# Cross-attention with sixteen heads and a routed feed-forward on one core: exponentials of 24 of 400 four-head steps on VectorE, eight passes with a spare PSUM bank, V stored once, half of the epilogue in the loop

## The chip, the cores and the metric

One core of a Trainium2 chip runs the whole program. The time is device microseconds of one execution; three runs of the kernel before gave 854.18, 855.53 and 856.58 us. One more execution, of 855.05 us, was profiled.

## The reference, cut to what matters

```python
def attention(query, key_value):            # 1024 x 128 queries (layer-normed x), 6404 x 96 context
    q, k, v = ...                           # 16 heads of 8 channels each
    attn = softmax(clip(einsum('bhqd,bhkd->bhqk', q, k) * 8 ** -0.5, -1e4, 1e4))
    return einsum('bhqk,bhkd->bqhd', attn, v) @ Wo + bo
def ffn(x):                                 # 1024 x 128, hidden 512, 8 experts, 2 taken
    main = gelu(x @ W1m + b1m) @ W2m + b2m
    gate_w, top_idx = top2(softmax(mean(x, 1) @ w_gate + b_gate))
    expert = sum over both of gate_w * (gelu(x @ W1e[i] + b1e[i]) @ W2e[i] + b2e[i])
    return a * main + (1 - a) * expert
x = x + attention(layernorm(x), ctx);  x = x + ffn(layernorm(x))
```

## The kernel before

**Opening.** The context is loaded, transposed on TensorE and projected to K and V. DVE splits K into a rounded part and a rest (`split_k`, ten segments of 5 key tiles of 128 keys), SP's queue stores the parts of a segment to `k_dram` (`store_k`, 2 DMAs) and loads them back in the order in which row-tiled matmuls want them (`load_k`, 8 DMAs, semaphore `kst_in[s]`). The same is done with Q (`load_q`, 16 DMAs for a group of four heads). There are two `kparts` buffers, and each load waits for the landing of its store. Segment 0 is handled ahead of the loop, segments 1 to 9 while the loop runs, in that order on SP's one queue, and after them the 32 small DMAs of the key tail (`load_k_tail`). A flag computed on the chip picks the fast path that is described here.

**Loop.** The 16 heads are four groups. A *step* is one key tile of 128 keys, four heads and 512 queries: four score matmuls (K=32 rows, on four row groups of the array, fp32r) give four chunks of 128x512 scores; ScalarE takes the exponential; four value matmuls (32 output columns each, on four column groups, fp32) add 8 value sums and the denominator of each head to a PSUM bank. Chunks are packed by three into a *tile* of 128x1536, for which PSUM has two buffers `ps` of three banks. Each group does 50 key tiles for both halves of the queries and a tail, which makes 134 tiles a group and 536 in all. The two remaining banks `po` hold the sums of the two halves. TensorE's order is written out: at tile t it issues the scores of tile t+2 once the exponential of tile t is done, and then the values of each step whose last chunk lies in tile t. ScalarE runs one ACTIVATE Exp per tile, with the scale and the bias as numbers in the instruction, into one of four `probs` buffers.

V is copied by DVE group by group into `region_v` with blocks of 32 columns per head (`refill`). The K of the next group is loaded over the old one segment by segment, once its scores are done. At the end of a group DVE copies the sums to `oraw`, TensorE turns them to tokens in a `ps` buffer, and DVE normalises (`group_to_tokens`, `normalise`).

**Epilogue.** In the last group the first half of the queries is finished early, and its output projection runs in the loop. After the loop stand the second half's projection, both layer norms, the first layer of the main network, the gate (with a table load for Exp), the loads of the two experts that were picked, their first and second layers, and the output. b2 is added by a matmul with one row for each of eight output tiles (L1010).

## Time and profile before

| | |
|---|---|
| median of three runs (lowest, highest) | 855.53 us (854.18, 856.58) |
| the profiled execution, its own time | 855.05 us |
| its span, from the first to the last instruction | 853.3 us |
| around the span | 1.75 us |
| busy ACT, PE, DVE | 775.5 us (91%), 751.9 us (88%), 80.0 us (9%) |
| exponentials of the loop (L430) | 536, busy 723.0 us, first at 55.15 us, over at 786.77 us |
| score and value matmuls of the loop | busy 268.9 us and 427.0 us |
| from the last exponential to the end | 66.5 us |

The busy time of an engine is the union of its instructions. An ACTIVATE is shown longer than the time between two starts, since neighbours overlap, so the cost of one in a stream is that distance. "Idle before" tells how long an engine stood and what released it.

### The profile page before, as it was taken

What the parts mean: (1) busy time and instruction counts of PE and PEld (TensorE: products, weight loads), DVE (VectorE), ACT (ScalarE), POOL (GpSimd) and SP (SyncE); (2) the same over time, 40 slices, a digit from 0 to 9 for tenths busy, and PEclk for the clock granted to TensorE, in tenths of its full rate; (3) what the DMA queues carried; (4) which work ended last, traced back from release to release, by engine and by line L of the source; (5) the groups of instructions that cost most, each with busy time, mean ns of one, the idle gap of its engine ahead of it and who ended that gap; (6) DMA issues with size and microseconds to landing.
All of it is one profiled execution on the core that took longest, in us unless ns stands there. A gap on an engine that the chain in (4) does not pass through costs nothing.

```text
span 853.3 us, 12912 instructions
## 1 busy us (share of the span) xinstructions
PE 751.9 (88%) x5352; PEld 241.4 (28%) x5352; DVE 80.0 (9%) x231; ACT 775.5 (91%) x636; POOL 21.8 (3%) x35
## 2 busy tenths in 40 slices
PE   3989888888898888888988888888988899888798
PEld 2652222222222222222222222222222223222467
DVE  6631220000010000000100000000100001000300
ACT  2769999999999999999999999999999999999450
POOL 9000000000000000000000000000000000000000
PEclk9999999999999999999999999999999999999799
DMA  5234441300011000011100011000000000000010
GB/s 176 82 103 121 118 130 25 81 16 16 17 41 28 20 17 17 16 24 24 36 21 16 17 22 26 16 17 16 17 1 1 2 1 1 1 1 1 3 50 25
DMA packets 20713, 29.04 MB, mean 34 GB/s; under 512 B 7830, under 2 KB 11276, under 8 KB 20652
## 3 DMA queue, kind: packets, MB, share of 16 engines
q1 hardware_dynamic: 19628, 27.40, 12.7%
q8 instruction: 44, 0.72, 0.4%
q0 software_dynamic: 480, 0.66, 0.3%
q10 hardware_dynamic: 544, 0.12, 0.1%
q14 instruction: 17, 0.14, 0.1%
HBM read 20.02 MB, written 8.13 MB: 33 GB/s over the span
## 4 chain that ended last, share of the span: by engine, by line
PE 42%; ACT 33%; issue 22%; DVE 1%; DMA 1%; SPq 0%; ACTq 0%
ACT region_ctxT L430 33%; PE po L913 19%; PE ps L894 12%; PE ps L995 3%; PE po L1007 3%; PE po L795 1%; PE ps L784 1%; DVE xn L514 1%; PE po L916 1%; DMA region_ctx<-in_ctx 1%; PE ps L772 1%; PE po L1010 0%; PE ps L896 0%; PE po L814 0%; PE ps L856 0%
## 5 line engine op out<-in xcount | busy, mean ns | idle before, releaser
L430 ACT ACTIVATE region_ctxT<-ps 128x1536 f32<-128x1536 f32 x536 | 723.0, 1675 | 8.6 <-PE ps L894 8.1
L913 PE MATMUL po<-region_ctxT,region_v 128*32 128x512 f32 x3200 | 427.0, 606 | 0.2 <-ACT region_ctxT L430 0.2
L894 PE MATMUL ps<-qst,region_k 32*128 32x512 f32 x1600 | 268.9, 493 | 76.1 <-ACT region_ctxT L430 75.9
L894 PEld LDWEIGHTS ps<-qst,region_k 32*128 32x128 f32 x1600 | 104.3, 181 | 445.8 <-ACT region_ctxT L430 436.9
L913 PEld LDWEIGHTS po<-region_ctxT,region_v 128*32 128x32 f32 x3200 | 63.0, 108 | 100.2 <-issue 97.3
L623 DVE COPY region_v<-vall 128x160 f32<-128x160 f32 x40 | 12.6, 318 | 405.8 <-PE po L913 402.5
L285 ACT ACTIVATE region_ctxT<-ps 96x512 f32<-96x512 f32 (+1 forms) x13 | 7.6, 582 | 13.5 <-PE ps L772 13.5
L772 PE MATMUL ps<-ident,region_ctx 128*96 128x128 f32 x50 | 9.4, 324 | 6.7 <-DMA region_ctx<-in_ctx 6.7
L658 DVE COPY region_kT<-po 128x512 f32<-128x512 f32 x2 | 1.4, 692 | 145.3 <-PE po L916 82.5
L784 PE MATMUL ps<-region_ctxT,wk_sb 96*128 96x512 f32 (+1 forms) x26 | 14.4, 652 | 0.0
L298 ACT ACTIVATE vall<-po 128x512 f32<-128x512 f32 (+1 forms) x13 | 7.5, 585 | 7.1 <-PE po L795 7.1
L995 PE MATMUL ps<-xnT,region_ctx 128*128 128x512 f32 x32 | 13.9, 592 | 0.0
L795 PE MATMUL po<-wv_sb,region_ctxT 97*128 97x128 f32 x100 | 12.7, 282 | 0.8 <-issue 0.5
L795 PEld LDWEIGHTS po<-wv_sb,region_ctxT 97*128 97x128 f32 x100 | 11.7, 191 | 2.1 <-issue 1.5
L459 ACT ACTIVATE region_v<-ps,b1s 128x512 f32<-128x512 f32 x8 | 5.5, 687 | 7.3 <-PE ps L995 7.3
L514 DVE TENSOR_SCALAR xn<-xres,mv,rstd 128x128 f32<-128x128 f32 x16 | 11.6, 1269 | 0.1
L995 PE MATMUL ps<-xnT,w1m_sb 128*128 128x512 f32 x16 | 10.1, 794 | 0.8 <-ACT xnT L446 0.8
L772 PEld LDWEIGHTS ps<-ident,region_ctx 128*96 128x96 f32 x50 | 7.1, 152 | 12.7 <-issue 9.3
L651 DVE COPY region_kT<-po 128x512 f32<-128x512 f32 x6 | 4.2, 692 | 59.4 <-PE po L916 59.4
L290 ACT ACTIVATE region_kT<-ps 128x512 f32<-128x512 f32 (+1 forms) x13 | 7.6, 587 | 2.2 <-PE ps L784 2.0
L1007 PE MATMUL po<-region_ctx,region_ctxT 128*128 128x128 f32 x64 | 9.2, 286 | 0.0
L543 DVE CAST kparts<-region_kT 128x640 fp32r<-128x640 f32 (+1 forms) x10 | 4.9, 491 | 43.5 <-DMA k_dram<-kparts 43.4
(163 smaller groups left out, 204.6 us busy)
## 6 DMA issues: line engine op xcount, KB each, us to landing
region_k<-k_dram SPq DMA_DIRECT2D x320, 40.0 KB, 1.9
k_dram<-kparts SPq DMA_DIRECT2D x18, 320.0 KB, 3.4
qst<-q_dram SPq DMA_DIRECT2D x64, 32.0 KB
region_ctx<-in_ctx SPq DMA_DIRECT2D x2, 624.0 KB, 8.5
q_dram<-region_k SPq DMA_DIRECT2D x2, 512.0 KB, 4.1
k_dram<-kparts SPq DMA_DIRECT2D x2, 322.0 KB, 3.3
region_ctx<-in_ctx SPq DMA_DIRECT2D x1, 576.0 KB, 6.8
xres<-in_x SPq DMA_DIRECT2D x1, 512.0 KB, 4.3
```

Source lines behind the costliest of these rows:

```text
L285: act.activation(ctxT[0:CK, a:b], bank(c % 3, CK, b - a), ACT.Copy).then_inc(ctxT_ready, 1)
L430: act.activation(probs[:, t % NPR, :], ps[slot_of_tile(t) % NSB][:, :], ACT.Exp, scale=SCALE).then_inc(exp_ready, 1)
L514: v.tensor_scalar(xn[:, t, :], xres[:, t, :], mv[:, t, 0:1], rstd[:, 3, t:t + 1], ALU.subtract, ALU.mult).then_inc(xn_ready, 1)
L623: v.tensor_copy(vst[:, t0:t1, :].rearrange("p t (j m) -> p t j m", j=GH)[:, :, :, 0:D], vall[:, t0:t1, g * GH * D:(g + 1) * GH * D].rearra ...
L772: last = tr(dst[:, at:at + P], ctx_sb[:, t, :], ident[:, :])
L784: mm(bank(3 + c % 3, P, b - a), wk_sb[:, :], ctxT[0:CK, a:b], start=True, stop=True).then_inc(k_psum, 1)
L795: last = mm(po[nth % 2][:, (t % 4) * P:(t % 4 + 1) * P], lhsT, wv_sb[:, :], start=True, stop=True)
L894: last = mm(dst, kst[r, kt * P:(kt + 1) * P], qst[r, g % 2, queries], start=True, stop=True)
L913: last = mm(po[half][QUAD * j:QUAD * (j + 1), :], vst[:, kt, QUAD * j:QUAD * (j + 1)], src, start=first, stop=last_one, skip_group_check=True)
L916: last = mm(po[half][:, :], vtail[:, :], src, start=first, stop=last_one, skip_group_check=True)
L995: mm(bank(n % 6), w, xnT[:, half * BANK:(half + 1) * BANK], start=True, stop=True).then_inc(hid_psum, 1)
L1007: last = mm(dst, hid[e % 2][:, cb, t * P:(t + 1) * P], w2[:, cb, :], start=(e == 0 and cb == 0 and t % 4 == 0), stop=False, skip_group_che ...
```

## The change

- **24 of the 400 steps** (`D_PLAN`: pass, key tile, the tiles at which its four score chunks are issued, the tile of its values) leave ScalarE. Their score matmuls go, one at a time and mostly four tiles apart, into the `po` bank that the current pass doesn't use, and DVE computes the exponential: `u` and `f` per chunk, and six instructions on a pair of chunks. ScalarE's tiles fall from 536 to 504.
- **Eight passes.** A pass is one group and one half of the queries, first all four groups for the first half, then again for the second. Sums alternate between the two `po` banks, and the other one is the spare bank; turning sums to tokens uses it too. K is loaded from `k_dram` seven times over instead of three, and all four groups of Q are kept (`load_q` for groups 1, 2 and 3 after segments 2, 3 and 4).
- **The constant C5** that DVE's polynomial leaves out is divided out of ScalarE's results too, by a bias in a tile `ebias` of 128x1. The scale moves in part into Q.
- **V once.** `evac_v` writes `v9`, 8 columns and a one per head, and values matmuls read 9 columns of it. `refill` goes. TensorE waits for the last V copy ahead of the first score.
- **Epilogue.** Projection, layer norm and the main network's first layer of the first half run in the loop, at tiles 255 to 266. Square roots and the gate's Exp become `pow` on POOL. The b2 sum is broadcast by one matmul and added by DVE to `xres`. The output is stored in three pieces.

```diff
+PASSES = [(g, half) for half in range(NHALF) for g in range(NG)]
+NP = len(PASSES)
+LAST_OF_HALF = [max(p for p, (_, h) in enumerate(PASSES) if h == half) for half in range(NHALF)]
...
+D_PLAN = [
+    (0, 49, (22, 26, 30, 34), 47),
+    (1, 24, (38, 42, 46, 50), 67),
+    (1, 34, (54, 58, 62, 70), 83),
...
+    (2, 24, (106, 110, 114, 118), 129),
...
+    (3, 34, (176, 180, 184, 194), 207),
...
+    (4, 24, (230, 234, 238, 242), 254),
+    (4, 39, (246, 272, 276, 280), 293),
...
+    (7, 49, (448, 452, 456, 460), 466),
+]
...
+STEPS = [(p, kt) for p in range(NP) for kt in range(FULL + 1) if kt not in DKT[p]]
+CHUNKS = [(n, j) for n, (_, kt) in enumerate(STEPS) for j in (range(GH) if kt < FULL else [None])]
+NT = len(CHUNKS) // CPT
...
+SPARE = sorted([(t, "score", GH * d + j) for d, (_, _, at, _) in enumerate(D_PLAN) for j, t in enumerate(at)]
+               + [(PASS_END[p] + NORM_GAP, "tokens", p) for p in range(NP - 1)])
...
+def pv_bank(p):
+    return p % 2
...
-                    if s == 2:
-                        load_q(sp, 1)
+                    if 2 <= s < 1 + NG:
+                        load_q(sp, s - 1)
...
-                for g in range(1, NG):
+                for p in range(1, NP):
                     for s in range(NSEG):
-                        chunks = (s + 1) * SEG_T * NHALF * GH if s < NSEG - 1 else CH_G
-                        sp.wait_ge(scores_ready, (g - 1) * TL_G + (chunks - 1) // CPT + 1)
-                        load_k(sp, g, s)
-                    if g + 1 < NG:
-                        load_q(sp, g + 1)
+                        sp.wait_ge(scores_ready, tile_of_segment(p - 1, s) + 1)
+                        if spare_of_segment(p - 1, s):
...
+                pool.memset(vtail[QUAD * j:QUAD * j + TAIL, :, QUAD * j + D:QUAD * j + V9], 1.0).then_inc(vones_ready, 1)
+            pool.wait_ge(vones_ready, 2 + GH)
+            pool.memset(powers[:, :], -0.5).then_inc(powers_ready, 1)
...
+            for n in range(NHALF):
+                pool.wait_ge(var_ready, 2 + n)
+                r = slice(n * QT // 2, (n + 1) * QT // 2)
+                pool.tensor_tensor(rstd[:, 3, r], rstd[:, 0, r], powers[:, 0:QT // 2], ALU.pow).then_inc(std_ready, 1)
+            pool.wait_ge(msum_ready, 2)
+            pool.tensor_tensor(gate[0:1, 2, :], euler[:, :], gate[0:1, 1, :], ALU.pow).then_inc(exp_gate, 1)
...
-                for t in range(NG * TL_G):
+                act.wait_ge(powers_ready, 3)
+                for t in range(NT):
                     act.wait_ge(scores_ready, t + 1)
                     if t >= NPR:
-                        g, i = divmod(t - NPR, TL_G)
-                        act.wait_ge(pv_done, g * QD_G + CHUNKS[g][CPT * i + CPT - 1][3] + 1)
-                    act.activation(probs[:, t % NPR, :], ps[slot_of_tile(t) % NSB][:, :], ACT.Exp, scale=SCALE).then_inc(exp_ready, 1)
+                        act.wait_ge(pv_done, values_through(t - NPR))
+                    act.activation(probs[:, t % NPR, :], ps[t % NSB][:, :], ACT.Exp, bias=ebias[:, 0:1],
+                                   scale=ESCALE).then_inc(exp_ready, 1)
+                if D_PLAN:
+                    act.wait_ge(d_ready, len(D_PLAN) * GH // 2)
...
+            act.wait_ge(pre_taken, CB)
+            act.activation(hid[0][:, :, 0:BANK], pre[:, :, :], ACT.Gelu_apprx_tanh).then_inc(main0_ready, 1)
...
+            def first_half_main(link):
+
+                take_first_attT()
+                residual(0, po[EPI_BANK][:, :], link)
+                dve.wait_ge(std_ready, 2)
+                scale_rows(halves[0])
+                dve.wait_ge(xnT_psum, NHALF + 1)
+                v.tensor_copy(xnT[:, 0:BANK], po[EPI_BANK][:, :]).then_inc(xnT_ready, 1)
+                dve.wait_ge(xnT_ready, NHALF + 1)
+                link(v.tensor_reduce(msum[:, 0:1], xnT[:, 0:BANK], AX.X, ALU.add))
+                for cb in range(CB):
+                    dve.wait_ge(pre_psum, cb + 1)
+                    v.tensor_scalar(pre[:, cb, :], po[EPI_BANK][:, :], b1T[:, E * CB + cb:E * CB + cb + 1], None,
+                                    ALU.add).then_inc(pre_taken, 1)
...
+                def take_sums(p):
+
+                    dve.wait_ge(pv_done, VALUES_OF_PASS[p][-1] + 1)
+                    v.tensor_copy(oraw[:, p % 2, :], po[pv_bank(p)][:, :]).then_inc(o_taken, 1)
...
+                    dve.wait_ge(spare_psum, n + 1)
+                    d_count(("u", c), v.tensor_scalar(du[:, i % 2, part], src, MAGIC, None, ALU.add))
+                    pair_until(i - 1, 1 + 3 * m)
+                    dve.wait_ge(d_step, d_mark["u", c])
+                    v.scalar_tensor_tensor(df[:, i % 2, part], du[:, i % 2, part], MAGIC, src,
+                                           ALU.subtract, ALU.subtract).then_inc(spare_taken, 1)
+                    pair_until(i - 1, 3 + 3 * m)
...
+                        if d_stage[i] == 1:
+                            dve.wait_ge(d_step, d_mark["u", 2 * i + 1])
+                            dve.wait_ge(spare_taken, SPARE_OF["score", 2 * i + 1] + 1)
+                            d_count(("e", i), v.tensor_scalar(u.bitcast(U32), u.bitcast(U32), 23, None, ALU.logical_shift_left))
...
+                            d_count(("q1", i), v.scalar_tensor_tensor(res, f, A1, f, ALU.add, ALU.mult))
+                        elif d_stage[i] == 3:
+                            d_count(("q2", i), v.scalar_tensor_tensor(q, f, A2, f, ALU.add, ALU.mult))
+                        elif d_stage[i] == 4:
+                            dve.wait_ge(d_step, max(d_mark["q1", i], d_mark["e", i]))
+                            d_count(("p1", i), v.scalar_tensor_tensor(res, res, B1, u, ALU.add, ALU.mult))
+                        elif d_stage[i] == 5:
+                            dve.wait_ge(d_step, max(d_mark["p1", i], d_mark["q2", i]))
+                            d_count(("p2", i), v.scalar_tensor_tensor(res, q, B2, res, ALU.add, ALU.mult))
+                        else:
+                            dve.wait_ge(d_step, d_mark["p2", i])
+                            v.scalar_tensor_tensor(res, f, R0, res, ALU.subtract, ALU.mult).then_inc(d_ready, 1)
...
+            dve.wait_ge(bsumb_psum, 1)
             for n in range(NHALF):
+                r = slice(halves[n].start, halves[n].stop)
+                v.tensor_tensor(xres[:, r, :], xres[:, r, :], bank(MIX_BANK)[:, P:2 * P].unsqueeze(1).broadcast_to([P, QT // 2, C]),
+                                ALU.add).then_inc(bsumb_taken, 1)
+            dve.wait_ge(bsumb_taken, NHALF)
+            for n, (t0, t1) in enumerate(OUT_TILES):
                 dve.wait_ge(ffn_psum, n + 1)
-                v.tensor_tensor(xn[:, n * QT // 2:(n + 1) * QT // 2, :],
-                                po[n][:, :].rearrange("p (t c) -> p t c", c=C),
-                                xres[:, n * QT // 2:(n + 1) * QT // 2, :], ALU.add).then_inc(res_ready, 1)
+                v.tensor_tensor(xn[:, t0:t1, :], [po[0], po[1], bank(4)][n][:, 0:(t1 - t0) * P].rearrange("p (t c) -> p t c", c=C),
+                                xres[:, t0:t1, :], ALU.add).then_inc(res_ready, 1)
...
+            def first_main(cb):
+
+                if cb == 0:
+                    pe.wait_ge(xnT_ready, NHALF + 1)
+                else:
+                    pe.wait_ge(pre_taken, cb)
+                mm(po[EPI_BANK][:, :], w1m_sb[:, cb * P:(cb + 1) * P], xnT[:, 0:BANK], start=True, stop=True).then_inc(pre_psum, 1)
...
+                    if (p, kt // SEG_T) not in seen:
+                        seen.add((p, kt // SEG_T))
+                        pe.wait_ge(kst_in[kt // SEG_T], 16 * GH * PARTS * (p + 1))
+                    r = slice(QUAD * j, QUAD * (j + 1))
+                    return mm(dst, kst[r, kt * P:(kt + 1) * P], qst[r, g, queries], start=True, stop=True)
...
+                def spare_job(n):
+
+                    t, kind, i = SPARE[n]
+                    if n:
+                        pe.wait_ge(spare_taken, n)
+                        if SPARE[n - 1][1:] == ("tokens", LAST_OF_HALF[0]):
+                            pe.wait_ge(pre_taken, CB)
+                    if kind == "tokens":
+                        pe.wait_ge(o_taken, i + 1)
+                        dst = po[1 - pv_bank(i + 1)]
+                        for a in range(QT // 2):
+                            last = tr(dst[:, a * P:(a + 1) * P], oraw[:, i % 2, a * P:(a + 1) * P], ident[:, :])
...
+                        d, j = divmod(i, GH)
+                        p, kt, _, _ = D_PLAN[d]
+                        last = scores(po[1 - pv_bank(pass_at(t))][:, :], p, kt, j)
+                    last.then_inc(spare_psum, 1)
...
+                    if first and p >= 1:
+                        used = sum(at <= t for at, _, _ in SPARE)
+                        if used:
+                            pe.wait_ge(spare_taken, used)
+                        if p >= 2:
+                            pe.wait_ge(o_taken, p - 1)
...
+                        if kind == 1:
+                            pe.wait_ge(d_ready, 2 * (i + 1))
+                        for j in range(GH):
+                            if kind == 0:
+                                tile, m = divmod(CHUNKS.index((i, j)), CPT)
+                                src = probs[:, tile % NPR, m * BANK:(m + 1) * BANK]
+                            else:
+                                src = dres[:, i % 2, j * BANK:(j + 1) * BANK]
+                            last = mm(dst[QUAD * j:QUAD * j + V9, :], v9[:, kt, GH * PASSES[p][0] + j, :], src,
...
+                pe.wait_ge(v_done, VCH)
+                pe.wait_ge(vones_ready, 1)
...
+                epilogue = PASS_END[LAST_OF_HALF[0]] + NORM_GAP
+                for t in range(NT):
+                    if t + NSB < NT:
                         score_tile(t + NSB)
+                    for n, (at, _, _) in enumerate(SPARE):
+                        if at == t:
+                            spare_job(n)
+                    if t == epilogue + EPI_AT[0]:
+                        pe.wait_ge(spare_taken, SPARE_OF["tokens", LAST_OF_HALF[0]] + 1)
+                        att_transpose(0, po[EPI_BANK])
+                    if t == epilogue + EPI_AT[1]:
+                        project_out(0, po[EPI_BANK])
+                    if t == epilogue + EPI_AT[2]:
+                        xn_transpose(0, po[EPI_BANK])
+                    if t - epilogue in EPI_AT[3:]:
+                        first_main(EPI_AT.index(t - epilogue) - 3)
```

Three places in the order of instructions, before and after. First **SP's queue** from the load of segment 2 (the second `region_k` group here) to the store of segment 5, before:

```order
L259 DMA region_k<-k_dram 16x640 x7
L280 DMA qst<-q_dram 8x1024 x16
L246 DMA k_dram<-kparts 16x8x640 [waits kparts_ready]
L246 DMA k_dram<-kparts 16x8x640
L259 DMA region_k<-k_dram 16x640 [waits kparts_stored1]
L259 DMA region_k<-k_dram 16x640 x7
L246 DMA k_dram<-kparts 16x8x640 [waits kparts_ready]
L246 DMA k_dram<-kparts 16x8x640
L259 DMA region_k<-k_dram 16x640 [waits kparts_stored0]
```

and now:

```order
L324 DMA region_k<-k_dram 16x640 x7
L343 DMA qst<-q_dram 8x1024 x16
L311 DMA k_dram<-kparts 16x8x640 [waits kparts_ready]
L311 DMA k_dram<-kparts 16x8x640
L324 DMA region_k<-k_dram 16x640 [waits kparts_stored1]
L324 DMA region_k<-k_dram 16x640 x7
L343 DMA qst<-q_dram 8x1024 x16
L311 DMA k_dram<-kparts 16x8x640 [waits kparts_ready]
L311 DMA k_dram<-kparts 16x8x640
L324 DMA region_k<-k_dram 16x640 [waits kparts_stored0]
L324 DMA region_k<-k_dram 16x640 x7
```

Behind the loads of segments 3 and 4 there now stand 16 more loads of Q each, ahead of the next store of K.

Second, **TensorE's queue** at the tiles 22 to 24 of the loop; `ps0` and `ps1` are the two score tiles, `po0` and `po1` the banks of sums. Before:

```order
L894 MATMUL ps0<-qst,region_k 128x512 x2
L894 MATMUL ps1<-qst,region_k 128x512 [waits exp_ready]
L894 MATMUL ps1<-qst,region_k 128x512 x2
L913 MATMUL po1<-region_ctxT,region_v 32x512 [waits exp_ready]
L913 MATMUL po1<-region_ctxT,region_v 32x512 x3
L894 MATMUL ps0<-qst,region_k 128x512 [waits exp_ready]
L894 MATMUL ps0<-qst,region_k 128x512 x2
L913 MATMUL po0<-region_ctxT,region_v 32x512 [waits exp_ready]
L913 MATMUL po0<-region_ctxT,region_v 32x512 x3
```

and now:

```order
L1022 MATMUL ps0<-qst,region_k 128x512 [waits exp_ready]
L1022 MATMUL ps0<-qst,region_k 128x512 x2
L1022 MATMUL po1<-qst,region_k 128x512 [waits kst_in9]
L1082 MATMUL po0<-region_ctxT,v9 9x512 [waits exp_ready]
L1082 MATMUL po0<-region_ctxT,v9 9x512 x3
L1022 MATMUL ps1<-qst,region_k 128x512 [waits exp_ready]
L1022 MATMUL ps1<-qst,region_k 128x512 x2
L1082 MATMUL po0<-region_ctxT,v9 9x512 [waits exp_ready]
L1082 MATMUL po0<-region_ctxT,v9 9x512 x3
L1022 MATMUL ps0<-qst,region_k 128x512 [waits exp_ready]
```

The score into `po1` is the first chunk of the first step of `D_PLAN`, key tile 49. It waits for `kst_in9`, and the values of tile 22 and all later scores of the loop stand behind it; the wait for `kst_in4` comes later in the queue.

Third, **TensorE's queue** at tile 38, now:

```order
L1022 MATMUL ps0<-qst,region_k 128x512 [waits kst_in6,exp_ready]
L1022 MATMUL ps0<-qst,region_k 128x512 x2
L1022 MATMUL po1<-qst,region_k 128x512 [waits kst_in4,qst_in1,spare_taken]
L1082 MATMUL po0<-region_ctxT,v9 9x512 [waits exp_ready]
L1082 MATMUL po0<-region_ctxT,v9 9x512 x3
L1022 MATMUL ps1<-qst,region_k 128x512 [waits exp_ready]
```

This chunk is the first of pass 1's key tile 24: it waits for the second load of segment 4, again ahead of the values and scores that follow. Before, no wait on that segment's second load stands ahead of the second group's own step.

**ScalarE's** exponential reads one more operand; before:

```order
L430 ACTIVATE region_ctxT<-ps0 128x1536 [waits pv_done,scores_ready]
```

and now:

```order
L501 ACTIVATE region_ctxT<-ps0,ebias 128x1536 [waits pv_done,scores_ready]
```

The operand `ebias` is the pointer to the 128x1 bias.

## Rows read from the trace of the kernel before

**Rows 1.** The page's costliest groups: busy us, mean ns of one, idle us before and its releaser.

```profile
L430 ACT ACTIVATE region_ctxT<-ps 128x1536 f32<-128x1536 f32 x536 | 723.0, 1675 | 8.6 <-PE ps L894 8.1
...
L894 PE MATMUL ps<-qst,region_k 32*128 32x512 f32 x1600 | 268.9, 493 | 76.1 <-ACT region_ctxT L430 75.9
```

**Rows 2.** Timeline of a steady stretch of the loop: start us, us, engine, line, count, idle before.

```profile
299.12 13.86 ACT L430 ACTIVATE region_ctxT<-ps 128x1536 f32<-128x1536 f32 x10
...
302.46 0.50 PE L894 MATMUL ps<-qst,region_k 32*128 32x512 f32 x3
...
302.90 1.07 PE L913 MATMUL po<-region_ctxT,region_v 128*32 128x512 f32 x8
```

**Rows 3.** Timeline of ScalarE in the opening, with pointer bias (L409, L411) and without.

```profile
26.53 0.68 ACT L411 ACTIVATE xn<-po,bqc 128x512 f32<-128x512 f32 x1
27.10 0.69 ACT L409 ACTIVATE qT<-po,bqc 128x512 f32<-128x512 f32 x1
...
28.33 0.59 ACT L285 ACTIVATE region_ctxT<-ps 96x512 f32<-96x512 f32 x1
28.81 0.60 ACT L290 ACTIVATE region_kT<-ps 128x512 f32<-128x512 f32 x1
```

**Rows 4.** Timeline of ScalarE in the epilogue, four Gelus with a pointer bias in a row.

```profile
809.50 2.42 ACT L459 ACTIVATE region_ctxT<-ps,b1T 128x512 f32<-128x512 f32 x4
```

**Rows 5.** Timeline of SP's queue: loads of K (L259), Q (L280), tail (L270), stores (L246).

```profile
65.46 3.55 SPq L259 DMA_DIRECT2D region_k<-k_dram  x8
69.06 5.40 SPq L280 DMA_DIRECT2D qst<-q_dram  x16
74.90 1.18 SPq L246 DMA_DIRECT2D k_dram<-kparts  x2
...
126.01 3.56 SPq L259 DMA_DIRECT2D region_k<-k_dram  x8
129.68 15.47 SPq L270 DMA_DIRECT2D ktail<-k_dram  x32
```

**Rows 6.** The page's DMA issues: KB each, us from issue to landing.

```profile
region_k<-k_dram SPq DMA_DIRECT2D x320, 40.0 KB, 1.9
```

**Rows 7.** Timeline where the loop begins.

```profile
54.70 0.49 ACT L298 ACTIVATE vall<-po 128x384 f32<-128x384 f32 x1 [0.55 <-PE po L795]
55.15 6.85 ACT L430 ACTIVATE region_ctxT<-ps 128x1536 f32<-128x1536 f32 x5
...
59.70 0.80 PE L894 MATMUL ps<-qst,region_k 32*128 32x512 f32 x3
...
60.43 1.94 PE L913 MATMUL po<-region_ctxT,region_v 128*32 128x512 f32 x8
...
63.01 4.22 ACT L430 ACTIVATE region_ctxT<-ps 128x1536 f32<-128x1536 f32 x3 [1.02 <-PE ps L894]
```

**Rows 8.** Windows: us, busy of PE, PEld, DVE, ACT, POOL, granted clock, DMA share, GB/s.

```profile
55.00:64.00 9.00, 6.75 (x45) 1.62 (x39) 3.33 (x7) 7.98 (x7) 0.00 (x0) 0.81 0.50 138
...
235.00:255.00 20.00, 18.41 (x133) 5.55 (x131) 3.04 (x9) 17.96 (x14) 0.00 (x0) 1.00 0.17 43
```

**Rows 9.** Groups by line and form, for the prices of DVE's work.

```profile
L535 DVE TENSOR_TENSOR region_k<-qT,region_k 128x1024 fp32r<-128x1024 f32 x1 | 1.2, 1226 | 0.0
...
L594 DVE TENSOR_TENSOR xres<-ps,xres 128x512 f32<-128x512 f32 x1 | 0.7, 692 | 4.0 <-PE ps L856 4.0
```

**Rows 10.** Timelines of the epilogue.

```profile
786.77 1.28 ACT L439 ACT_TABLE_LOAD   x1
...
806.60 1.28 ACT L471 ACT_TABLE_LOAD   x1
...
816.98 13.90 PE L995 MATMUL ps<-xnT,region_ctx 128*128 128x512 f32 x32
...
840.35 0.48 PE L1010 MATMUL po<-bsum,ones 1*128 1x128 f32 x2
...
840.76 1.16 PE L1007 MATMUL po<-region_ctx,region_ctxT 128*128 128x128 f32 x8
```

482 lines of the change are left out of this document (253 added, 229 removed).

## The prediction

> **What bounds the kernel now.** I read the page's costliest groups first. The loop's 536 exponentials are busy for 723.0 us, 1.349 us each, and ScalarE stood only 8.6 us before them; TensorE stood 76.1 us before its scores, nearly all of it for ScalarE [rows 1]. The loop is ScalarE's, by a small margin. The timeline of a steady stretch shows the margin: ten exponentials span 13.86 us. Taking off the last one's own length (the mean of 1.675 us in [rows 1], a little more here) leaves 1.34 to 1.35 us from start to start [rows 2], and I use 1.343. TensorE takes 0.44 us from its scores to its values, and the values of a step last 1.07 us, of which some 0.07 overlap with what follows [rows 2]. Four tiles carry three steps: 4 x 0.44 + 3 x 1.00 = 4.8 us against ScalarE's 5.37. So whoever takes work from ScalarE must leave its other tiles as fast as they are, and must not stop TensorE, whose queue is in order. Both are to be tested.
>
> **1. Fewer exponentials.** 32 tiles of 1.343 us go: 43.0 us less. This is the intended gain.
>
> **2. Each exponential gets dearer.** The instruction now reads its bias through a pointer. The trace has ScalarE with and without one, at 512 elements and in a stream: from L411 to the next L409, both with a pointer, 0.57 us from start to start; from L285 to L290, without, 0.48 [rows 3]. Four Gelus with a pointer take 2.42 us, (2.42 - 0.69) / 3 = 0.577 from start to start [rows 3, 4]. 512 elements are the same in all, so 0.09 us is per instruction, and nothing hides it, since ScalarE is the bound. Bounds: 0 (if the long instruction hides the read, as it already starts before its neighbour ends) and 0.097. I take 0.09, because the rows are of streams as well. 504 x 1.433 = 722.2 us, against 536 x 1.343 = 719.8: the gain of part 1 is used up.
> The Trainium skill's page "ScalarE: Activation LUTs", section "What ACT_TABLE_LOAD costs", gives an ACTIVATE without pointers 186 ns + 0.833 ns per element, about 93 ns more per pointer operand, and an overlap of about 93 ns between neighbours. By it one would cost an estimated 1.466 us and the loop some 17 us more than I sum; the trace has less distance than that today, so the measured one decides.
>
> **3. TensorE waits for a K segment that isn't there yet.** The spare score at tile 22 is key tile 49, in segment 9, and needs its first load. In the trace the loads of segment 9 are issued from 126.01 us on for 3.56 us, and a load lands 1.9 us after issue: there at about 131 us [rows 5, 6]. SP's queue sets this, with one segment after another through store, landing and load. It now has two more Q loads ahead: from the Q load at 69.06 to the next store at 74.90 are 5.84 us [rows 5], so 11.7 us twice over, less 0.2 us for the `refill` that DVE no longer has in front. Segment 9 is there at 142.6 us. When is tile 22? The first score waits for the last V copy, which ends at 54.70 + 0.49 = 55.2 us; with scores behind it the first exponential starts at 55.9 instead of 55.15 [rows 7]. The exponential of tile 22, after which the spare score stands, is over at 55.9 + 23 x 1.433 = 88.9 us, and with the scores that are already there ScalarE runs through tile 24 until 91.7. Then the values and scores behind the spare score have to come: at the low clock 0.5 + 1.94 + 0.8 us, as at the loop's start [rows 7], where the granted clock was 0.81 in the mean of a window [rows 8], thus partly at 1.2 GHz. Tile 25 starts at 145.5: **53.8 us** of idle ScalarE. Segments 4 to 8 arrive meanwhile, so nothing more waits in pass 0.
>
> **4. A second such wait.** At tile 38 the score of pass 1's key tile 24 wants the second load of segment 4. Behind segment 9, SP has the key tail, 129.68 + 15.47 us in the trace [rows 5], shifted by 11.5: until 156.7. Five segments of 3.55 us follow, until 174.4, landed at 175.9. TensorE has the scores through tile 40 issued, and ScalarE ends tile 40 at 145.5 + 1.0 (TensorE still cold, 1.02 us were lost so before [rows 7]) + 16 x 1.433 = 169.4; tile 41 starts at 178, and 1 us is lost again. Together **10.5 us** with the 1.0 of the first restart. The later spare scores come 6 to 36 tiles (8.6 us and more) after the scores that release their segment, and a load takes 3.55 + 1.9 us: no wait.
>
> **5. TensorE's margin.** Four tiles are now 5.73 us long, and hold 4.8 us as before, one spare score (0.2 to 0.43 us, from a third of [rows 2]'s 0.50 to all of it) and a quarter of a step's values (0.25): 5.2 to 5.5 us. It fits, but not evenly: 19 of the 24 steps put their values in a tile that has values already, 2.4 us of work in one tile. I take 0.2 us each, **5** (0 to 12). Each pass ends with a tail chunk and transposes. Three group ends cost 20.00 - 17.96 = 2.0 us each [rows 8]; seven ends with half the work, four of them with first values that wait for DVE's normalise in the same tile, I take at **8** (3 to 14) in all. Half an epilogue in the loop: transposes, projection and four 512-column matmuls of 0.86 us (13.90 us for 16 pairs [rows 10]) are some 6.4 us in 14 tiles that have 3.3 to spare: **3** (1 to 6).
>
> **6. DVE.** Per chunk it does two instructions from PSUM of 512 elements (0.69 us each) and three of 1024 (1.23 us each [rows 9]): at most 5.1 us in 5.73. ScalarE's loop hides it. If this cover goes, each 0.1 us over costs 9 us. Nine instead of 32 weight columns change nothing, since 512 columns are streamed as before and a step's four matmuls keep their four column groups; seven K loads instead of three lie beside the loop. Both cost nothing.
>
> **7. The end.** From the last exponential to the end are 66.5 us (853.3 - 786.8 [rows 10]). Up to the second half's layer norm all stays. Then TensorE is no longer in the first half's first layer, and the gate loses a table load of 1.28 us at 806.60 [rows 10] and gets POOL's `pow` instead, of which there is no row; I take it at half the table load, with 0 and 2 us as bounds. The experts' first layer, at 816.98, can start 2.7 us (1 to 4) sooner, when its weights have landed. Eight b2 matmuls go, 840.35 to 840.76 each [rows 10]: 3.3 us, and up to 4.7 without the breaks in the stream, I take 4.0. A smaller last output gives 0.3. End: **59.5 us** (57 to 63).
>
> **Sum.** 55.9 + 722.2 + 53.8 + 10.5 + 5 + 8 + 3 = 858.4 us for the loop's end; + 59.5 = 917.9 us of span; + 1.75 us around the span, as in the profiled execution of 855.05 us, gives **919.7 us**. That execution is 0.5 us under the median of 855.53, so I leave it at that.
>
> **Rivals.**
> A. The pointer's read is hidden in long instructions. For it: exponentials last 1.675 us and follow each other at 1.343, so 0.3 us overlap. Against it: [rows 3, 4]. Then 45.3 us less, the two waits begin sooner and last 3.6 us longer, and TensorE at 5.2 to 5.5 us of 5.37 becomes the bound, some 10 us: **888 us**.
> B. K arrives in time; the place is `kst_in9` at tile 22. For it: today TensorE waits for ScalarE alone ahead of its scores [rows 1]. Against it: the queue's dates, which no term of the change brings forward. It decides from the point at which segment 9 is there by 91.7 us; each us sooner gives one back, 64.3 in all: **855 us**, and with part 5's terms at their low ends 843, faster than before.
> C. DVE's chain of waits on its own results makes a chunk 6.2 us instead of at most 5.1: ScalarE waits by way of the spare bank in some 90 intervals, + 0.47 x 90: **962 us**. Against it: DVE's start gaps are small, and independent instructions lie between.
> D. The change does what it says, A and B at once: 919.7 - 64.3 - 45.3 + 10 = **820 us**.
>
> **How the numbers follow.** Forecast 0.74, A 0.10, B 0.04, C 0.08, D 0.02, and 0.02 for something else that is slower. The forecast's own range is 905 to 934, from the bounds in parts 2 to 7. To hold 8 in 10 the range must take in the better part of A: 884 to 934. About 0.3% is what this kernel's measurement can tell from no change: 853 to 858 us. Faster: D and half of B, 0.04; same: 0.02; slower: the rest, 0.94.
>
> **What the profile of the changed kernel would show.** Part 2: the exponential's busy time over its 504 instructions, 1.43 us against 1.349. Parts 3 and 4: two idle stretches of ScalarE, of some 54 and 9 us, released by a spare score that was released by a load of K; segment 9's loads issued until 141 us. Part 5: ScalarE's other idle time before L501 around 16 us. Part 6: DVE at 80 to 90% in the loop, with TensorE's waits on it short. Part 7: 59 to 60 us behind the last exponential. It would be wrong if SP's queue ran ahead of its dates, or if the pointer were free.

## The result, and the profile after

The changed kernel takes **923.53 us** (median of 4 runs, 923.22 to 925.35) against 855.31 us for the kernel before (4 runs): the ratio is 1.080, with a 95% interval of 1.078 to 1.082. The forecast was 919.7 us, the range 884 to 934. The profiled execution took 925.35 us, 1.8 us over the median, with a span of 923.6 us; the steps below are measured against the forecast span of 917.9 us.

The page's costliest groups of the kernel after (line, engine, operation, count, busy us, mean ns of one, idle us before and its releaser) answer to [rows 1]:

```profile
L501 ACT ACTIVATE region_ctxT<-ps,ebias 128x1536 f32<-128x1536 f32 x504 | 726.4, 1615 | 84.7 <-PE ps L1022 83.5
...
L1022 PE MATMUL po<-qst,region_k 32*128 32x512 f32 x96 | 40.4, 421 | 59.1 <-DMA region_k<-k_dram 59.1
```

Busy time over count is 726.4 / 504 = 1.441 us for an exponential, against 1.349 in [rows 1], and ScalarE's idle time before them has gone from 8.6 to 84.7 us. The second row is the spare scores: 59.1 us of TensorE's idle time before them, all for a load of K. The timeline of ScalarE (start us, length us, count, idle before and its releaser) shows where the idle time lies:

```profile
51.82 5.83 ACT L501 ACTIVATE region_ctxT<-ps,ebias 128x1536 f32<-128x1536 f32 x4 [0.66 <-PE ps L1022]
...
140.89 1.54 ACT L501 ACTIVATE region_ctxT<-ps,ebias 128x1536 f32<-128x1536 f32 x1 [50.96 <-PE ps L1022]
143.44 21.58 ACT L501 ACTIVATE region_ctxT<-ps,ebias 128x1536 f32<-128x1536 f32 x15 [1.01 <-PE ps L1022]
175.43 1.54 ACT L501 ACTIVATE region_ctxT<-ps,ebias 128x1536 f32<-128x1536 f32 x1 [10.41 <-PE ps L1022]
177.87 11.56 ACT L501 ACTIVATE region_ctxT<-ps,ebias 128x1536 f32<-128x1536 f32 x8 [0.90 <-PE ps L1022]
...
344.50 23.01 ACT L501 ACTIVATE region_ctxT<-ps,ebias 128x1536 f32<-128x1536 f32 x16 [0.28 <-PE ps L1022]
...
811.63 1.54 ACT L501 ACTIVATE region_ctxT<-ps,ebias 128x1536 f32<-128x1536 f32 x1 [3.44 <-PE ps L1022]
```

Two stretches, 50.96 us until 140.89 and 10.41 us until 175.43, are the forecast's waits for K. Each has a restart behind it (1.01 and 0.90 us). Sixteen exponentials in a row take 23.01 us and a lone one 1.54, so from start to start it is (23.01 - 1.54) / 15 = 1.431 us. In TensorE's timeline, the instruction that ends each wait is a spare score, and the matmuls behind it are slow:

```profile
137.50 0.79 PE L1022 MATMUL po<-qst,region_k 32*128 32x512 f32 x1 [49.81 <-DMA region_k<-k_dram]
138.22 1.90 PE L1082 MATMUL po<-region_ctxT,v 128*9 128x512 f32 x8
...
143.63 1.05 PE L1082 MATMUL po<-region_ctxT,v 128*9 128x512 f32 x8
...
172.07 0.76 PE L1022 MATMUL po<-qst,region_k 32*128 32x512 f32 x1 [9.29 <-DMA region_k<-k_dram]
```

The values of a step take 1.90 us there, as at the loop's start in [rows 7], against 1.05 a few microseconds later. Between 90 and 137 us TensorE did nothing and its granted clock was 0.50, that is 1.2 GHz. It was still 0.50 from 138 to 143 us, where the slow matmuls are, and from 185 us on it is 1.00 (windows: us, busy of PE, PEld, DVE, ACT, POOL, granted clock, DMA share, GB/s):

```profile
90.00:137.00 47.00, 0.00 (x0) 0.00 (x0) 6.96 (x20) 0.00 (x0) 0.00 (x0) 0.50 0.48 122
138.00:143.00 5.00, 5.00 (x24) 0.95 (x25) 1.38 (x2) 1.54 (x1) 0.00 (x0) 0.50 0.03 1
...
185.00:860.00 675.00, 597.73 (x4440) 151.54 (x4436) 426.55 (x499) 656.15 (x457) 1.04 (x1) 1.00 0.15 32
```

SP's queue (L311 stores of K, L324 loads of K, L343 of Q, L335 of the key tail) answers to [rows 5]. Three groups of Q loads of 5.4 us stand between K's segments (at 64.42, 79.46 and 92.51 us), where one stood before, and the loads of segment 9 begin at 132.40 instead of 126.01. The second loads of K follow from 152.01 us on:

```profile
79.46 5.38 SPq L343 DMA_DIRECT2D qst<-q_dram  x16
...
92.51 5.38 SPq L343 DMA_DIRECT2D qst<-q_dram  x16
...
132.40 3.55 SPq L324 DMA_DIRECT2D region_k<-k_dram  x8
...
152.01 44.82 SPq L324 DMA_DIRECT2D region_k<-k_dram  x64
```

### The profile page after: what moved, and what is told of

It is laid out like the page before. It is cut to its first block, busy times and chain, and to the rows that moved or that the text cites. A ratio compares the mean times of both kernels' runs of the same rounds, so it can differ in the third digit from the quotient of the medians.

```text
span 923.6 us, 13620 instructions
## 1 busy us (share of the span) xinstructions
PE 752.6 (81%) x5338; PEld 228.6 (25%) x5338; DVE 498.4 (54%) x669; ACT 772.9 (84%) x591; POOL 20.7 (2%) x37
## 4 chain that ended last, share of the span: by engine, by line
ACT 33%; PE 27%; issue 25%; SPq 7%; DMA 5%; DVE 3%; POOLq 0%; ACTq 0%; POOL 0%; DVEq 0%
ACT region_ctxT L501 33%; PE po L1082 12%; PE ps L1022 6%; SPq L324 5%; DMA k_dram<-kparts 3%; PE ps L1157 2%; SPq L343 2%; PE po L1176 1%; PE ps L914 1%; PE po L925 1%; PE po L1071 1%; DMA region_ctx<-in_ctx 1%; PE po L1022 1%; PE ps L902 1%; SPq L311 1%
## 5 line engine op out<-in xcount | busy, mean ns | idle before, releaser
L501 ACT ACTIVATE region_ctxT<-ps,ebias 128x1536 f32<-128x1536 f32 x504 | 726.4, 1615 | 84.7 <-PE ps L1022 83.5
L1082 PE MATMUL po<-region_ctxT,v 128*9 128x512 f32 x3008 | 399.1, 603 | 3.8 <-ACT region_ctxT L501 3.8
L736 DVE TENSOR_SCALAR region_kT<-po 128x512 f32<-128x512 f32 x96 | 66.4, 692 | 196.3 <-PE po L1022 196.3
L1022 PE MATMUL po<-qst,region_k 32*128 32x512 f32 x96 | 40.4, 421 | 59.1 <-DMA region_k<-k_dram 59.1
L1082 PEld LDWEIGHTS po<-region_ctxT,v 128*9 128x9 f32 x3008 | 44.8, 88 | 107.1 <-issue 96.3
L739 DVE SCALAR_TENSOR_TENSOR region_kT<-region_kT,po 128x512 f32<-128x512 f32 x96 | 65.3, 681 | 0.2
L770 DVE SCALAR_TENSOR_TENSOR dres<-region_kT,dres 128x1024 f32<-128x1024 f32 x48 | 58.8, 1225 | 1.6
L767 DVE SCALAR_TENSOR_TENSOR dres<-region_kT,dres 128x1024 f32<-128x1024 f32 x48 | 58.5, 1220 | 0.2
L759 DVE SCALAR_TENSOR_TENSOR dres<-region_kT 128x1024 f32<-128x1024 f32 x48 | 58.5, 1219 | 0.0
L761 DVE SCALAR_TENSOR_TENSOR region_kT<-region_kT 128x1024 f32<-128x1024 f32 x48 | 58.5, 1218 | 0.0
L764 DVE SCALAR_TENSOR_TENSOR dres<-dres,region_kT 128x1024 f32<-128x1024 f32 x48 | 58.4, 1216 | 0.0
L608 DVE CAST kparts<-region_kT 128x640 fp32r<-128x640 f32 (+1 forms) x10 | 4.9, 492 | 60.1 <-DMA k_dram<-kparts 59.1
L457 POOL TENSOR_TENSOR rstd<-rstd,powers 128x4 f32<-128x4 f32 x2 | 2.1, 1026 | 855.7 <-DVE rstd L562 855.7
```

What stands on the lines that cost most here:

```text
L501: act.activation(probs[:, t % NPR, :], ps[t % NSB][:, :], ACT.Exp, bias=ebias[:, 0:1], scale=ESCALE).then_inc(exp_ready, 1)
L736: d_count(("u", c), v.tensor_scalar(du[:, i % 2, part], src, MAGIC, None, ALU.add))
L739: v.scalar_tensor_tensor(df[:, i % 2, part], du[:, i % 2, part], MAGIC, src, ALU.subtract, ALU.subtract).then_inc(spare_taken, 1)
L759: d_count(("q1", i), v.scalar_tensor_tensor(res, f, A1, f, ALU.add, ALU.mult))
L761: d_count(("q2", i), v.scalar_tensor_tensor(q, f, A2, f, ALU.add, ALU.mult))
L764: d_count(("p1", i), v.scalar_tensor_tensor(res, res, B1, u, ALU.add, ALU.mult))
```

## The experiments

The theory was that of the prediction: the pointer eats the 32 exponentials that were saved, and SP's queue of loads makes TensorE, and with it ScalarE, wait twice. In the figures below, "the changed kernel" takes 923.5 us and the kernel before between 854.5 and 855.7 us, measured anew beside each set of runs.

### The pointer alone, in the kernel before

```diff
+            pool.memset(zbias[:, :], 0.0).then_inc(zbias_ready, 1)
...
-                    act.activation(probs[:, t % NPR, :], ps[slot_of_tile(t) % NSB][:, :], ACT.Exp, scale=SCALE).then_inc(exp_ready, 1)
+                    act.activation(probs[:, t % NPR, :], ps[slot_of_tile(t) % NSB][:, :], ACT.Exp, bias=zbias[:, 0:1], scale=SCALE).then_inc(exp_ready, 1)
```

> The kernel before, with one edit: its 536 exponentials read their bias (zero) through a pointer to a column of 128 values, as in the changed kernel. Theory (part 2: the read costs 0.09 us for each instruction, nothing hides it): stream spacing 1.343 -> 1.433 us, 536 x 0.09 = 48 us, 903 us in all (855 to 907 by the bounds). Rival A (the read is hidden in the long instruction): 855 us, within 0.3%.

Measured: **898.54 us** (896.03 to 899.07), ratio 1.052 (1.050 to 1.055). The page's row for the exponentials:

```profile
L434 ACT ACTIVATE region_ctxT<-ps,zbias 128x1536 f32<-128x1536 f32 x536 | 768.8, 1878 | 7.1 <-PE ps L898 7.1
```

768.8 / 536 = 1.434 us against 1.349. The 43.9 us between the medians are 0.082 us for each exponential, 0.080 to 0.087 by the interval. The timelines have 128 exponentials in one piece, first with the pointer, then in the kernel before:

```profile
261.42 183.41 ACT L434 ACTIVATE region_ctxT<-ps,zbias 128x1536 f32<-128x1536 f32 x128 [0.60 <-PE ps L898]
```

```profile
63.01 172.13 ACT L430 ACTIVATE region_ctxT<-ps 128x1536 f32<-128x1536 f32 x128 [1.02 <-PE ps L894]
```

Taking off a lone one's length (1.54 and 1.45 us), these are 1.432 and 1.344 us from start to start, 0.088 apart. So the price taken from instructions a third as long, 0.09 us, was right to 0.002 us for the distance in a stream, and 10% too high for the time. Part of the difference is idle time of ScalarE, which falls from 8.6 to 7.1 us; the rest wasn't taken apart. The pointer's read is not hidden in a long instruction, and rival A's condition is false. By the Trainium skill, page "ScalarE: Activation LUTs", section "What ACT_TABLE_LOAD costs", a pointer operand adds about 93 ns: the 0.088 us agree to within 0.01 us. Its level of 1.466 us does not: this run shows 1.432.

### The pointer taken out of the changed kernel

The added lines are POOL's; TensorE takes `v9d` instead of `v9` for the values of VectorE's steps.

```diff
-                    act.activation(probs[:, t % NPR, :], ps[t % NSB][:, :], ACT.Exp, bias=ebias[:, 0:1],
-                                   scale=ESCALE).then_inc(exp_ready, 1)
+                    act.activation(probs[:, t % NPR, :], ps[t % NSB][:, :], ACT.Exp, scale=ESCALE).then_inc(exp_ready, 1)
...
+            for i, kt in enumerate(DK):
+                pool.tensor_scalar(v9d[:, i, :, :], v9[:, kt, :, :], C5, None, ALU.mult).then_inc(v9d_ready, 1)
```

> The changed kernel without the pointer: the exponentials have no bias again, and the factor that the bias stood for is put on copies of V's columns for the six key tiles that VectorE's steps use. Theory (the pointer costs 0.082 us, as in the kernel before with a pointer, and the K waits' dates don't move, so that the 41 exponentials ahead of tile 41 gain nothing): 463 x 0.082 = 38 us less, 886 us, and up to 10 us more if TensorE becomes the bound at 5.2 to 5.5 us for four tiles of 5.37 (range 885 to 896). Rival (in the changed kernel ScalarE's spacing is set by something else, such as TensorE or DVE, and the pointer is hidden): 915 us or more.

Measured: **896.59 us** (895.62 to 897.16), 26.9 us less and just above the range. The rows of ScalarE, first the page's, then two of the timeline:

```profile
L504 ACT ACTIVATE region_ctxT<-ps 128x1536 f32<-128x1536 f32 x504 | 684.9, 1523 | 96.1 <-PE ps L1024 94.4
...
140.06 1.45 ACT L504 ACTIVATE region_ctxT<-ps 128x1536 f32<-128x1536 f32 x1 [52.45 <-PE ps L1024]
...
357.90 21.60 ACT L504 ACTIVATE region_ctxT<-ps 128x1536 f32<-128x1536 f32 x16 [0.63 <-PE ps L1024]
```

The exponentials' busy time falls by 726.4 - 684.9 = 41.5 us, 0.082 each (0.085 in the first experiment, and 0.088 here too from start to start: (21.60 - 1.45) / 15 = 1.343). Their idle time rises from 84.7 to 96.1 us. The two K waits (now 52.45 and 11.81 us) take 2.5 us of it with their restarts, since they end only 0.8 and 1.1 us sooner. The wait for the last step's values and its restart take 1.9 us (4.49 + 1.10 against 3.44 + 0.29). The other 7 us are TensorE's margin: behind most of VectorE's steps ScalarE stands about 0.6 us, where it stood 0.28 with the pointer (the 0.28 at 344.50 above). Rival A's 10 us for this were about right, and that the price comes in the tiles of a step's values too.

### Only the first step's key tile changed

```diff
-    (0, 49, (22, 26, 30, 34), 47),
+    (0, 4, (22, 26, 30, 34), 47),
```

> The changed kernel, with the key tile of the first VectorE step changed from 49 (segment 9) to 4 (segment 0, in place long before tile 22). Theory (the load queue on SP is the limit, and both waits are its dates): the 51 us wait at tile 22 goes, and the wait for segment 4's second load at tile 38, whose date (loaded from 172, ScalarE on again at 175) no edit here moves, grows from 10 to some 60 us: 920 to 923 us, less than 0.5% faster than the changed kernel. Rival (each wait is the cost of its own key tile, parts 3 and 4 add up): 51 us less, 872 us.

Measured: **924.00 us** (923.08 to 924.95), no gain at all. TensorE's waits of 50 to 200 us (what was waited for: us in total, times, longest us), and VectorE's and TensorE's timelines:

```profile
PE po L1022 <- DMA region_k<-k_dram: 30.3, 1, 30.3
PE po L1022 <- DVE region_kT L739: 23.3, 1, 23.3
...
117.39 0.83 DVE L609 TENSOR_TENSOR kparts<-region_kT,kparts 128x644 fp32r<-128x644 f32 x1
...
121.08 0.69 DVE L736 TENSOR_SCALAR region_kT<-po 128x512 f32<-128x512 f32 x1
...
171.48 0.76 PE L1022 MATMUL po<-qst,region_k 32*128 32x512 f32 x1 [30.32 <-DMA region_k<-k_dram]
```

The wait for segment 9 is gone. The second one lasts 30.3 us and ends at 171.48, where it ended at 172.07 before: SP's queue sets that date, as the theory has it. But there is a wait of 23.3 us that no part of the prediction has, for VectorE. The second spare score needs the bank that VectorE has to empty first, and VectorE's own queue is in order: all its splits of K (L608, L609, until 118.2 us), then `add_bo` and the tail's copies, and only at 121.08 the first instruction of its exponentials. So tile 26 has to wait for VectorE until 121 us whatever the key tile is. In the changed kernel VectorE is free from 121.4 us on, and the first spare score comes at 137.50: this wait lies wholly inside that for segment 9, and no row shows it.

### The Q loads on another queue

```diff
-                    if 2 <= s < 1 + NG:
-                        load_q(sp, s - 1)
...
+            pool.wait_ge(qparts_stored, 16 * PARTS)
+            for g in range(1, NG):
+                load_q(pool, g)
```

> The changed kernel, with the Q loads of groups 1 to 3 issued by POOL instead of between K segments on SP. Theory: three times 5.4 us leave SP's queue ahead of segment 9 (or of the key tail), so that both dates come 16 us sooner: ScalarE on again at 125 and 159 us, in all 907 us (905 to 909). Rival (DVE's splitting or the round trip through DRAM sets segment 9's date, not the queue): 918 to 923 us. A second rival: POOL's own issuing slows DVE down, which would show in DVE's split instructions.

Measured: **909.39 us** (907.72 to 911.27), 14.1 us less. ScalarE's timeline has the two waits end where they were expected, at 125.0 and 159.2 us, where they ended at 140.89 and 175.43:

```profile
125.00 1.54 ACT L502 ACTIVATE region_ctxT<-ps,ebias 128x1536 f32<-128x1536 f32 x1 [34.74 <-PE ps L1023]
...
159.22 13.25 ACT L502 ACTIVATE region_ctxT<-ps,ebias 128x1536 f32<-128x1536 f32 x9 [10.90 <-PE ps L1023]
```

Both dates come from SP's queue, and what is taken out of it ahead of them is gained nearly in full. VectorE's instructions are as long as before (its 96 readings of the spare bank take 692 ns in both), so POOL's issuing costs it nothing there.

### A table of steps without a wait for K

With the Q loads on POOL, the second step moved to pass 0 and the next ones behind tile 74:

```diff
-    (0, 49, (22, 26, 30, 34), 47),
-    (1, 24, (38, 42, 46, 50), 67),
-    (1, 34, (54, 58, 62, 70), 83),
-    (1, 49, (74, 78, 82, 86), 99),
+    (0, 4, (22, 26, 30, 34), 47),
+    (0, 24, (38, 42, 46, 50), 63),
+    (1, 4, (74, 78, 82, 86), 99),
...
-    (7, 49, (448, 452, 456, 460), 466),
+    (7, 49, (450, 454, 458, 462), 475),
+    (7, 48, (466, 470, 474, 478), 491),
```

> The changed kernel with the Q loads on POOL as in the run before this one, and with a table of VectorE steps of which none asks for a segment that is not there: the first two in pass 0 on key tiles 4 and 24, the next ones in pass 1 from tile 74 on, the later ones up to 16 tiles later than in the changed kernel, the last one's values 12 tiles before the end instead of at the first tile possible. 24 steps and 504 exponentials as in the changed kernel. Theory: both K waits (62.9 us with their restarts) and the 3.4 us wait for the last step's values go: 857 us (854 to 864; up to 7 more if the second load of segment 0, at tile 66, comes late instead). Rival (the waits hide other costs, contention of DVE with TensorE or the margin of TensorE, that surface when they are gone): 870 us or more.

Measured: **866.46 us** (865.58 to 872.26), still 1.3 to 2.1% above the kernel before. The K waits and the wait at the last step are gone, 57 us, but it is 9 us more than expected:

```profile
110.27 1.54 ACT L502 ACTIVATE region_ctxT<-ps,ebias 128x1536 f32<-128x1536 f32 x1 [15.89 <-PE ps L1023]
...
106.88 0.79 PE L1023 MATMUL po<-qst,region_k 32*128 32x512 f32 x1 [14.75 <-DVE region_kT L740]
...
105.41 0.69 DVE L737 TENSOR_SCALAR region_kT<-po 128x512 f32<-128x512 f32 x1
```

15.89 us of idle ScalarE and 1.01 at the restart behind it are VectorE's splits again, seen here with nothing over them: the splits end at 102.5 us, a scaling, `add_bo` and the tail's copies follow in VectorE's queue, the first exponential of VectorE starts at 105.41, the spare score of tile 26 at 106.88.

### The first step behind VectorE's splits

A new table: the first step's spare scores at tiles 38 to 50, the second's from 71 on, 24 steps as before.

```diff
-    (0, 4, (22, 26, 30, 34), 47),
-    (0, 24, (38, 42, 46, 50), 63),
+    (0, 4, (38, 42, 46, 50), 63),
+    (1, 9, (71, 75, 79, 83), 96),
+    (1, 39, (87, 91, 95, 99), 112),
```

> As the run with a new table of steps (Q loads on POOL, no step on a segment that isn't there), but with the first VectorE step at tiles 38 to 50 instead of 22 to 34, behind DVE's last split of K (102.5 us there), and the others behind it without the old gaps; 24 steps and 504 exponentials still. Theory (DVE does all splits of K before its first exponential, so the second spare score of a step at tile 22 waits for DVE until 103 us): the 15.9 us wait and its restart of 1.0 us go, 849 us (847 to 853). Rival (K's arrival is what bounds pass 0 there, by 7.6 us for each segment against 9.5 us of use, and the wait only moves): 860 us or more.

Measured: **858.43 us** (856.06 to 860.17). The wait is gone, for good: the exponentials run from 61.45 to 147.6 us in one piece. Of the 17 us expected only 8 came, and ScalarE's timeline shows what took most of the rest:

```profile
61.45 86.14 ACT L502 ACTIVATE region_ctxT<-ps,ebias 128x1536 f32<-128x1536 f32 x60 [0.27 <-PE ps L1023]
...
428.30 5.83 ACT L502 ACTIVATE region_ctxT<-ps,ebias 128x1536 f32<-128x1536 f32 x4 [2.12 <-PE ps L1023]
...
707.21 1.54 ACT L502 ACTIVATE region_ctxT<-ps,ebias 128x1536 f32<-128x1536 f32 x1 [3.03 <-PE ps L1023]
...
702.81 0.69 DVE L719 COPY region_kT<-po 128x512 f32<-128x512 f32 x1
...
PE po L1045 <- DVE region_kT L719: 4.1, 2, 2.2
```

VectorE is busy with a step's chunks when it should copy the pass's sums (L719); the transposes (L1045) wait for that copy, 4.1 us in two places, and TensorE's queue behind them. The idle 3.03 and 2.12 us are that. At 707.21 the last spare score stands two tiles ahead of the transposes; the tables of the changed kernel and of the run before have it at least five tiles ahead. That distance isn't the whole cause: at 428.30 it is seven tiles, and VectorE is still busy with that step's instructions until the copy at 425.38. By the profiles 1.5 us more are in the end behind the last exponential, 61.3 against 59.8 us; this comes back in "Without the pointer and without the waits".

### Values in empty tiles, and free tiles ahead of a pass's end

A third table: every step's values in a tile with no other values, and no spare score in the four tiles ahead of the transposes.

```diff
-    (0, 4, (38, 42, 46, 50), 63),
-    (1, 9, (71, 75, 79, 83), 96),
-    (1, 39, (87, 91, 95, 99), 112),
+    (0, 4, (38, 42, 46, 50), 64),
+    (1, 4, (71, 75, 79, 83), 95),
+    (1, 34, (87, 91, 95, 99), 111),
...
-    (7, 39, (440, 445, 449, 453), 466),
-    (7, 49, (457, 461, 465, 469), 482),
+    (7, 49, (455, 459, 463, 467), 481),
+    (7, 48, (471, 475, 479, 483), 497),
```

> As the run whose first VectorE step is at tile 38 (858.4 us; pointer kept, Q loads on POOL), with a third table of steps: each step's values stand in a tile that has no other values (16 of 24 stood in one that has), and no spare score stands in the four tiles ahead of a pass's transposes, so that DVE is free to copy the sums. Theory (part 5: a step's values in a tile that has values cost ScalarE 0.28 us, and the pass ends of 2.1, 3.0, 1.3 and 0.7 us are DVE being late with the copy of the sums): 16 x 0.28 = 4.5 and some 4 us less, 850 us (848 to 853). Rival (TensorE's margin is used up in the mean, wherever the values stand): 856 us or more.

Measured: **852.30 us** (849.91 to 854.06), ratio to the kernel before 0.997 (0.995 to 0.998). ScalarE's idle time before the exponentials is down from 17.9 to 13.3 us, 4.6 us less where some 8.5 were expected, and whole passes (63 exponentials) run in one piece:

```profile
L502 ACT ACTIVATE region_ctxT<-ps,ebias 128x1536 f32<-128x1536 f32 x504 | 724.5, 1736 | 13.3 <-PE ps L1023 12.9
...
152.60 90.49 ACT L502 ACTIVATE region_ctxT<-ps,ebias 128x1536 f32<-128x1536 f32 x63 [0.88 <-PE ps L1023]
```

One wait of 2.64 us is left at a pass end (at 615.88). So with the pointer, and without the waits for K and for the splits, the change is worth 0.3%.

### Without the pointer and without the waits

The second table with the key tail's loads on POOL too and without the pointer, then the same with the third table:

```diff
-                load_k_tail(sp)
...
+            load_k_tail(pool)
```

> The run before it and, in addition, no pointer (the factor on copies of V's columns for eight key tiles) and the key tail's loads on POOL behind the Q loads, so that the second load of segment 0 comes before tile 64. Theory: 504 x 0.082 = 41 us less than the run before it, and 3 to 10 us more for TensorE as the bound: 814 us (808 to 820). Rival (TensorE, with 4.8 us of its own and spare scores and VectorE's values in 5.37 us, is over its margin by more): 825 us or more.

Measured: **824.12 us** (822.96 to 825.29), 34.3 us less than the run that it starts from, with 41.4 us less of busy exponentials for the pointer (725.2 us in that run, 683.8 in the page below) and 9.4 us more of idle time (27.3 against 17.9). The time expected was 10 us too low because the run that it starts from was expected at 849.

> The 824.1 us run (no pointer, Q and key tail loads on POOL) with this third table of steps. Theory: at 1.343 us for a tile a step's values in a tile that has values cost 0.63 us and the late copies at the pass ends some 6 us: 16 x 0.63 = 10 and 4 to 6 us less, of which TensorE's mean of 22.2 us in 16 tiles against 21.5 gives some back: 811 us (806 to 817). Rival (TensorE is the bound in the mean): 820 us or more.

Measured: **821.01 us** (819.76 to 821.65), 10 us more than expected. By the page, first the one, then the other:

```profile
L505 ACT ACTIVATE region_ctxT<-ps 128x1536 f32<-128x1536 f32 x504 | 683.8, 1534 | 27.3 <-PE ps L1025 27.0
```

```profile
L505 ACT ACTIVATE region_ctxT<-ps 128x1536 f32<-128x1536 f32 x504 | 685.1, 1526 | 19.2 <-PE ps L1025 18.6
```

The idle time falls by 8.1 us, not by the 14 to 16 expected. Of the 0.6 us behind each step nothing is left (62 exponentials run in one piece, from 503.57 us on), but 3.90 us still stand at one pass end, where VectorE copies the sums late, although the last spare score is seven tiles ahead of the transposes there. Of the 8.1 us, 3.9 arrive in the span (3.1 between the medians): the exponentials begin 1.4 us later in this execution (52.94 against 51.55), are busy 1.3 us longer, and the end behind them is 1.5 us longer. Most of that last part is in the first 16 matmuls of the experts' first layer, in the timelines of the one and the other:

```profile
790.25 8.83 PE L1162 MATMUL ps<-xnT,region_ctx 128*128 128x512 f32 x16 [2.88 <-DMA b2rows<-in_b2e]
```

```profile
785.24 10.02 PE L1162 MATMUL ps<-xnT,region_ctx 128*128 128x512 f32 x16 [2.94 <-DMA b2rows<-in_b2e]
```

TensorE's granted clock was 0.71 in the mean of the first 6 us of this stretch, then 0.51; the same 16 matmuls take 7.13 us at a clock of 1.00, in the run of the third table with the pointer. TensorE stood 2.5 us before them there, and 2.9 here. So up to 2.9 us of an execution's end are the clock, and a difference of that size between two runs isn't the edit's. The time, 821 us, is what the rival asked for (820 or more), but its mechanism isn't seen: between 500 and 590 us TensorE is busy for 83.5 of 90 us and ScalarE runs without a break from 503.57 to 587.7 us. The margin left is small, since those 62 exponentials follow at (84.14 - 1.45) / 61 = 1.356 us instead of 1.343.

### The change without VectorE's steps

```diff
+D_PLAN = []
...
-                    act.activation(probs[:, t % NPR, :], ps[t % NSB][:, :], ACT.Exp, bias=ebias[:, 0:1],
-                                   scale=ESCALE).then_inc(exp_ready, 1)
+                    act.activation(probs[:, t % NPR, :], ps[t % NSB][:, :], ACT.Exp, scale=ESCALE).then_inc(exp_ready, 1)
```

> The change without its VectorE steps: no key tile goes to VectorE, so 536 exponentials and no spare scores, no pointer, Q and key tail loads on POOL; V stored once, eight passes, the spare bank's transposes and the first half's epilogue in the loop as in the change. Theory: first exponential at 51.5, 536 x 1.343 = 719.8, start, pass ends and epilogue 10 to 12, end 61, + 1.75: 845 us (843 to 849), so that the 24 steps are worth some 34 of their 43 us, and all the rest of the change 9 to 10 us. Rival (the eight passes and the epilogue in the loop cost as much as the shorter end gives): 855 us.

Measured: **850.53 us** (848.36 to 851.13), ratio 0.994 (0.992 to 0.996).

```profile
L476 ACT ACTIVATE region_ctxT<-ps 128x1536 f32<-128x1536 f32 x536 | 724.1, 1677 | 12.7 <-PE ps L996 12.7
```

This places the parts. All but VectorE's steps (V stored once, eight passes, the spare bank, half an epilogue in the loop, fewer matmuls at the end; here also with the Q and key tail loads on POOL) brings 4.4 us, where I had expected 9 to 10: 12.7 us of idle time instead of 8.6, nearly all at pass ends (0.4 to 0.5 us, twice each) and in the epilogue, and 724.1 us of exponentials where 719.8 were expected. Against it, the run at 821.0 us puts VectorE's 24 steps at 29.5 us of the 43.0 that 32 exponentials are long. Of the gain without them, 3.5 us are an earlier first exponential (51.68 against 55.15 us), which the next section explains.

### VectorE's scaling and a memset on POOL

The changed kernel's first exponential starts 3.3 us sooner than before (51.82 against 55.15 in [rows 7]), where the prediction has it 0.75 us later. VectorE's scaling of the first layer norm is shorter: 4.97 us after, 9.37 before. In the kernel before it stands beside a memset of the whole V region, which the change replaces by a small one. VectorE's and POOL's timelines of the kernel before, and two of the eight instructions by themselves, the fourth and the fifth, which overlap:

```profile
11.91 9.37 DVE L514 TENSOR_SCALAR xn<-xres,mv,rstd 128x128 f32<-128x128 f32 x8
...
14.90 5.45 POOL L381 MEMSET region_v<- 128x6400 f32 x1
...
12.68 7.82 DVE L514 TENSOR_SCALAR xn<-xres,mv,rstd 128x128 f32<-128x128 f32 x2
```

```diff
+            pool.wait_ge(xn_ready, QT)
             pool.memset(region_v[:, :], 0.0).then_inc(vones_ready, 1)
```

> The kernel before, with one edit: POOL's memset of the whole V region (5.45 us) waits until DVE's layer norm has scaled all eight tiles. Theory (while that memset runs, DVE's scaling stands still, 9.37 instead of 4.97 us, and everything behind it waits): 4 us less, 851 us (ratio 0.995). Rival (something else lengthens the scaling, or ScalarE's evacuations set that stretch): 855 us, within 0.2%.

Measured: **847.11 us** (844.57 to 848.80), ratio 0.991 (0.989 to 0.993), 7.4 us less:

```profile
13.34 2.14 DVE L515 TENSOR_SCALAR xn<-xres,mv,rstd 128x128 f32<-128x128 f32 x8
```

The eight instructions take 2.14 us with the memset behind them (it starts at 15.54 us), and 7.2 us fewer here are 7.4 in the time, where 4 were expected: this stretch is on the path. In the kernel before, the two scalings end at 20.50 us, 0.15 us after the memset (20.35). They stand still from 12.68 on, though, 2.2 us before the memset starts in the trace, and in the changed kernel two of them last from 12.92 to 14.82 us, where the memset starts only at 14.94. POOL's spans are rough, and what holds them that early stays open; POOL's DMA issues, which fill its time from 12.62 to 14.91 us, stand beside the eight scalings in this run too and don't slow them. The Trainium skill has a rule for such pairs on its page "SBUF — State Buffer", section "Who interferes with whom": VectorE in a two-port mode, which `tensor_scalar` can enter, and GpSimd share a pair of ports, and whoever issues first has it for the whole instruction. The trace agrees in the common end, 20.50 and 20.35 us. By its starts VectorE was first, at 12.68 against 14.90 us, and would not have had to wait: that part of the rule isn't borne out by it.

The same edit in the fastest version:

> The 821.0 us run with one more edit: POOL's memset of V's ninth columns (1.6 us) waits until DVE's layer norm has scaled its eight tiles. Theory (the edit that gave 7.4 us in the kernel before, where a 5.4 us memset lay on the scaling): the scaling falls from 5.23 to 2.14 us, 3 us less, 818 us (817 to 819.5). Rival (a 1.6 us memset does not matter, and other accesses lengthen the scaling): 821 us.

Measured: **815.19 us** (813.68 to 816.42), ratio to the kernel before **0.953** (0.951 to 0.955), the fastest of all. VectorE's scaling takes 2.14 us here too. The gain is 5.8 us instead of 3: the first exponential starts at 47.28 instead of 52.94. Of these 5.7 us, 3.1 are the scaling's (5.23 against 2.14 us). Of the other 2.6, 2.5 are TensorE's clock: the transposes and projections next in its queue take from 18.11 to 23.60 us in the run at 821.0, for the most part at 1.2 GHz, behind waits for the scaling, and from 14.91 to 17.92 here, at 2.4 GHz. These are the windows of the one and the other:

```profile
18.00:24.00 6.00, 6.00 (x16) 3.15 (x15) 1.65 (x3) 2.59 (x7) 0.19 (x2) 0.58 0.00 0
```

```profile
15.00:20.00 5.00, 5.00 (x22) 2.80 (x21) 2.15 (x4) 3.95 (x10) 2.62 (x9) 1.00 0.07 24
```

The four query projections, for one, take 3.08 us there and 1.88 here. The whole edit against the changed kernel is: no pointer, Q and key tail loads on POOL, the third table, and this wait.

## Why the prediction was right, and where its steps were off

**The kernel is slower by the mechanism forecast.** The 32 exponentials are paid back by the pointer, and two waits for K come on top. The span's account, measured against forecast:

- Start of the loop: 51.8 against 55.9 us, **-4.1**. The step that was off is in part 3, where the first exponential's date is carried over from before with 0.75 us added. V stored once also takes a large memset off POOL, and that was holding up VectorE; a smaller one still does in the changed kernel.
- Part 2, 504 exponentials: 726.4 us busy against 722.2, **+4.2**. In a stream they follow at 1.431 us, as forecast (1.433). But a lone one takes 1.54 us (the row at 140.89), so each of the 43 pieces of the stream costs 0.11 us beside its idle time: 504 x 1.431 + 43 x 0.11 = 725.9 us. The sum had no term for this.
- Parts 3 and 4, the K waits with their restarts: 63.3 against 64.3 us, **-1.0**. ScalarE runs again at 140.9 and 175.4 us, where 145.5 and 178 were forecast. SP's queue is 5.1 us earlier at segment 9 than forecast (132.40 against 126.01 + 11.5). Of these 3.7 are the earlier start (the loads of segment 0 at 41.08 against 44.75 us), and 1.4 are the two Q loads, which delay it by 10.1 and not by 11.5 us. The lengths, 51 against 53.8 and 10.4 + 1.9 against 10.5, hold but for one thing: behind the second wait TensorE was counted at its full clock, 2.1 us from the landing to ScalarE's start, and it was at 0.50 there as well, 3.4 us (172.07 to 175.43). The recorded 145.5 is also 0.3 us less than its own terms give, 142.6 + 0.5 + 1.94 + 0.8.
- Part 5 and the restart of the loop: 20.8 us of other idle time against 16, **+4.8**. The start of the loop, 1.9 us of breaks behind the first six exponentials, was in no part. The half epilogue took 4.9 us in seven breaks, not 3, and pass ends and VectorE's steps together 10.5, not 13. Missing is the wait of 3.44 us at 811.63. The last line of `D_PLAN` asks for its values six tiles after its last spare score, where the others have some 13, and VectorE isn't done. The prediction speaks of the later steps' segments there, and not of the time between a spare score and its values.
- Part 7, the end: 61.35 against 59.5 us, **+1.9**. The experts' first layer starts 2.1 us sooner, not 2.7, and what follows is 3.0 us shorter, not 4.3. POOL's two `pow` are 1.01 and 1.63 us; the second is the term that the prediction took at half a table load, 0.64. The larger part is a term that the prediction doesn't have, TensorE's clock. In the changed kernel the experts' first 16 matmuls take 8.83 us, with the clock at 0.72 from 890 to 896 us, and in the run of the third table 7.13, with the clock at 1.00; that run's end is 59.8 us. The 66.5 us of before hold such a stretch as well: eight matmuls of the main network take 6.45 us there, at a clock of 0.56, and 3.70 with the pointer in the kernel before, at 1.00, whose end is 63.3 us. So the clock is on both sides of this part, and its small error is in part luck.

Together +5.8 us, from 917.9 to 923.6; the median lies 1.8 us below that execution, so the forecast of 919.7 is 3.8 us short.

```profile
808.97 1.89 PE L1082 MATMUL po<-dres,v 128*9 128x512 f32 x8 [2.00 <-DVE dres L770]
...
875.01 1.01 POOL L457 TENSOR_TENSOR rstd<-rstd,powers 128x4 f32<-128x4 f32 x1 [374.50 <-DVE rstd L562]
880.62 1.63 POOL L459 TENSOR_TENSOR gate<-euler,gate 1x8 f32<-1x8 f32 x1 [4.60 <-DVE gate L853]
...
890.32 8.83 PE L1157 MATMUL ps<-xnT,region_ctx 128*128 128x512 f32 x16 [2.69 <-DMA b2rows<-in_b2e]
```

And the same matmuls in the run of the third table:

```profile
817.17 7.13 PE L1158 MATMUL ps<-xnT,region_ctx 128*128 128x512 f32 x16 [2.52 <-DMA b2rows<-in_b2e]
```

**Part 6** had VectorE 80 to 90% busy; it is 426.6 of 675 us, 63%, between 185 and 860 us. The bound of 5.1 us for a chunk was sound (4.8 by the page's means), but a chunk doesn't come every four tiles. That it is hidden holds in the loop. It does not hold at the start: this is the mechanism that the prediction missed altogether. It asked when a K segment is there, and never when VectorE is free, whose queue has nine splits of K, each waiting for a store, ahead of its first exponential. It cost nothing to the forecast, only because a longer wait lies over it.

**The rivals.** A's condition, a hidden pointer, is refuted by two runs; its size for a kernel without the pointer's cost, 888 us, was 8.6 us too low. B asked for segment 9 by 91.7 us, and put each microsecond of earlier arrival at one microsecond of time. The first 16 us obey that (14.1 measured). The whole doesn't: in the run with K in time, VectorE's splits kept 16.9 us of it, so that 855 us was too low for B. C's 6.2 us for a chunk doesn't occur. D, with both, was put at 820 us; the run that fulfils it measures 821.0, with a table of steps that also heeds the splits and the pass ends. That the two numbers are so close is luck: in this run the first exponential is 3 us sooner than in the sum, the exponentials are busy 8 us longer, the idle time is 7 us less and the end 3.5 us longer.

**Open** is what holds VectorE's scaling from 12.68 us on, and why TensorE's clock falls in the end of some executions and not of others. Whether the splits of K could be spread between VectorE's exponentials, so that a step at tile 22 pays, wasn't tried.

## What to carry to other kernels

When work is moved to an engine with time to spare, ask at which date that engine, and the data, are free for the first piece, not only how busy it is in the mean: a queue in order turns one early piece into an idle stretch of the engine that you meant to relieve. A long wait can hide a shorter one (23.3 us under 49.8 here), so take a cause away alone and look at what ends the idle time then, before you add up gains. And an operand that a formula seems to give away, here a bias through a pointer, has its price times the number of instructions: 0.082 us by 504 is 41 us, nearly all of the 43 us that the change was to gain.

## What the hardware showed that I had not expected

- Two of eight `tensor_scalar` of 128x128 on VectorE, which take 0.27 us each in the mean (2.14 us for eight), lasted until 7.8 us after their start and ended with a POOL memset of 5.45 us; moving that memset made the whole kernel 7.4 us faster. Such a stall costs more than its length where TensorE stands for it: 5.7 us for a stall of 3.1, with a clock of 0.58 behind it instead of 1.00 (the last two runs of this document).
- The same 16 matmuls near the end took 7.13, 8.83 or 10.02 us, at a granted clock of 1.00, about 0.72 and 0.51 in their first 6 us.
- A lone exponential of 1536 columns with a pointer takes 1.54 us and one in a stream comes every 1.43; without a pointer it is 1.45 and 1.343. So breaks in a stream cost beyond their idle time.
- POOL's `pow` took 1.01 us for 128x4 and 1.63 us for 1x8 elements, so their total number (512 and 8) doesn't set it. The number in a partition (4 and 8) might; two sizes can't tell.
